# First edge layer of a four-layer graph network: the two column parts of an edge sum resized, and the tail copy placed behind the weighing

## The chip, the cores and the metric

One core of a Trainium2 chip runs the whole program. The metric is the device time of one execution in microseconds. The engines are named as the profile names them: PE is TensorE (PEld its weight loads), DVE is VectorE, ACT is ScalarE, POOL is GpSimd, SP is SyncE.

## The reference

The network has four layers of message passing over 625 nodes and 20000 edges, each followed by a feed-forward or mixture-of-experts part. The change touches the first attention layer of the first of them:

```python
def gatv2(x, src, dst, Ws, bs, Wd, bd, attn):
    H, D = attn.shape                       # 8 heads x 96 here
    fs = (x @ Ws + bs).reshape(-1, H, D)
    fd = (x @ Wd + bd).reshape(-1, H, D)
    e = jax.nn.leaky_relu(fs[src] + fd[dst], 0.2)
    logits = jnp.einsum('ehd,hd->eh', e, attn)
    m = jax.ops.segment_max(logits, dst, num_segments=N)
    ex = jnp.exp(logits - m[dst])
    denom = jax.ops.segment_sum(ex, dst, num_segments=N)
    alpha = ex / denom[dst]
    out = jax.ops.segment_sum(alpha[:, :, None] * fs[src], dst, num_segments=N)
    return jax.nn.elu(out)
```

What concerns us is `logits`: for each edge, the source row and the target row are added (768 columns), passed through a leaky ReLU, multiplied by `attn` and summed in 8 heads of 96 columns.

## The kernel before

The edges are sorted into 181 tiles (`ES`) of up to 128 edges, so that all sources of a tile lie in one block of 125 nodes and all targets in one block. A loop over the 181 tiles computes their logits; it runs twice, once for each of the two attention layers of this part (`first_edges` with g = 0, and `second_edges` with g = 1). Each node row has 776 columns (`GW`): 768 features and 8 columns with a part of the logits that needs no ReLU (the linear 0.2 share, already summed by head). These 8 are called the tail.

One pass of the first loop, for tile i:

- TensorE adds one tally matmul (L826) to a table that counts edges between nodes. Then `node_rows` (L799) picks the source and the target rows with one-hot matrices: four matmuls (two sides, each in a large and a small part) into the PSUM area zA, which holds the last columns with the tail, and four into zB, which holds the first 512 columns. zA shares its PSUM bank with the last part of the tally, so its matmuls always add to what lies there (`first=False`), and it must be cleared before each pass. There is one zA and one zB.
- ScalarE copies the 8 tail columns out of zA (L1272), builds the one-hots of tile i+2 in two steps (`turned_gap`, L1251, the absolute distance of the node number; `turned_onehot`, L1257), and clears zA by copying zeros into it (L1277).
- VectorE weighs the last columns (`weigh_end`, L1725: the larger of 0 and the sum, times the attention vector, into a product buffer), sums the product of the tile before by head (L1735), weighs the first columns from zB (`weigh_start`, L1730), builds a one-hot for every second tile (L1740), and every fourth pass finishes the logits of four tiles (`finish`, L1717).
- GpSimd builds the one-hots of the tally six tiles ahead (L679, L680) and scatters the finished logits to a table in memory (L692). SyncE loads the target numbers of eight tiles at a time, spread over the partitions, into two buffers.

The order is written out by hand for each engine's queue, and semaphores tie the queues: `s_za` counts zA sums, `s_tc` tail copies, `s_wa` weighings of zA, `s_zr` clearings, `s_zp` zB sums, `s_mul` weighings of zB, `s_hd` head sums, `s_tg` gaps and `s_tt` one-hots. The tally matmul of tile i waits for `s_zr` at i; the zB matmuls wait for `s_mul` at i; the tail copy waits for `s_za`; `weigh_end` waits for `s_tc`; the clearing waits for `s_wa`. In the second loop each tile has one of four PSUM areas of two banks, nothing is cleared, and the parts are 384 and 392 columns wide.

Of the kernel before, what the change touches and what calls it, by code (L numbers as in the profile page):

```python
# [14 lines left out]
ALU = mybir.AluOpType  # L15
AX_X = mybir.AxisListType.X

P = 128
# [4 lines left out]
D = 768  # L23
# [7 lines left out]
ES = (E + NQ * (P - 1)) // P  # L31
EW = -(-ES // 4) * 4
HB = D // 2
NB = 16
GW = D + 8
FF = 3072
# [84 lines left out]
def build(nc, ins, out):  # L121
    ctx = ExitStack()
    with ctx:
        def sb(name, shape, dt=F32):
            return ctx.enter_context(nc.sbuf_tensor(name, shape, dt))
# [41 lines left out]
        PB = sb("PB", [P, 3840])  # L167
# [4 lines left out]
        NEG = sb("NEG", [P, T, N])  # L172
# [94 lines left out]
        prod = [WB[:, 2048 + D * b:2048 + D * (b + 1)] for b in range(2)]  # L267
# [35 lines left out]
        PS = ctx.enter_context(nc.psum_tensor("PS", [P, 8, 512], F32))  # L303
        PSz = PS[:, :, :].rearrange("p b n -> p (b n)")
        zw = [PS[:, 2 * b:2 * b + 2, :] for b in range(4)]
        zA = PS[:, 6, P:P + GW - 512]
        zB = PS[:, 7, 0:512]
        tallied = PSz[:, 0:NQ * P]


# [15 lines left out]
        s_za = sem("first_columns_added")  # L326
        s_wa = sem("first_columns_weighed")
        s_tt = sem("turned_onehots_ready")
        s_zp = sem("target_rows_added")
# [24 lines left out]
        s_tc = sem("linear_parts_copied")  # L354
        s_zr = sem("last_columns_cleared")
# [4 lines left out]
        s_mul = sem("edge_products_ready")  # L360
# [401 lines left out]
        def _(pe):  # L762
# [32 lines left out]
            def node_rows(out, i, cd, cs, a, b, first=True):  # L795

                for side, c in ((0, cs), (1, cd)):
                    for part in (large, little):
                        mm = pe.matmul(out, ohT[i % 3][:, (1 - side) * P:(2 - side) * P],  # L799
                                       part[side][:, bass.ds(c, 1), a:b].rearrange("p o n -> p (o n)"),  # L800
                                       start=first, stop=side == 1 and part is little, skip_group_check=True)
                        first = False
                return mm

            def first_edges():

                pe.wait_ge(s_line, 2 * T * 2)
                pe.wait_ge(s_zero, 1)
                for bank in (2, 3, 4, 5, 6, 0, 1):
                    if bank == 0:  # L810
                        pe.wait_ge(s_sorted, 1)
                    if bank == 1:
                        pe.wait_ge(s_idc, 1)
                    pe.matmul(PS[:, bank, :], NEG[:, 0, 0:P], iota[:, 0:512], start=True, stop=False,
                                   skip_group_check=True)
                pe.wait_ge(s_lo, 2 * T)
                now, then = None, blocks_of(0)
                for i in range(ES):
                    if i % 4 == 0:
                        now = then  # L820
                    cs, cd = now[i % 4]
                    wait(pe, s_zr, i)
                    pe.wait_ge(s_oh, i + 1)
                    if i % 2:
                        pe.wait_ge(s_odd, i // 2 + 1)
                    pe.matmul(tallied[:, bass.ds((cd * T + cs) * P, P)], oht[i % 8], ohs[i % 8], start=False,  # L826
                              stop=i == ES - 1, skip_group_check=True).then_inc(s_ohu, 1)
                    pe.wait_ge(s_tt, i + 1)
                    node_rows(zA, i, cd, cs, 512, GW, first=False).then_inc(s_za, 1)
                    if i % 4 == 1 and i // 4 + 1 < EW // 4:  # L830
                        then = blocks_of(i // 4 + 1)
                    wait(pe, s_mul, i)
                    node_rows(zB, i, cd, cs, 0, 512).then_inc(s_zp, 1)
                pe.wait_ge(s_cnt, 1)

            def second_edges():
# [377 lines left out]
        def _(act):  # L1214
# [26 lines left out]
            def edge_parts(g):  # L1241

                chunks = -(-ES // CH)

                def turned_gap(i):
                    q = g * chunks + i // CH
                    if i % CH == 0:
                        act.wait_ge(s_idb[q % 2], 16 * (q // 2 + 1))
                    if i >= 2:
                        act.wait_ge(s_tt, ES * g + i - 1)  # L1250
                    act.activation(tgap[i % 2][0:R], spread_ids[q % 2][0:R, i % CH * 2 * P:(i % CH + 1) * 2 * P],  # L1251
                                   ACT.Abs, bias=node[0:R], scale=-1.0).then_inc(s_tg, 1)

                def turned_onehot(i):
                    act.wait_ge(s_tg, ES * g + i + 1)
                    wait(act, s_zp, ES * g + i - 2)
                    act.activation(ohT[i % 3], tgap[i % 2][0:R], ACT.Relu, bias=ones[0:R, 0:1],  # L1257
                                   scale=-1.0).then_inc(s_tt, 1)

                turned_gap(0)  # L1260
                turned_gap(1)
                turned_onehot(0)
                turned_onehot(1)
                for i in range(ES):
                    if g == 0:
                        act.wait_ge(s_za, i + 1)
                    else:
                        act.wait_ge(s_zp, ES * g + i + 1)
                    if i >= EU:
                        act.wait_ge(s_lg, -(-ES // 4) * g + i // 4 - 2)  # L1270
                    tail = zA[:, D - 512:GW - 512] if g == 0 else zw[i % 4][:, 1, HB:GW - HB]
                    act.copy(tails[:, i % EU, :], tail).then_inc(s_tc, 1)  # L1272
                    if i + 2 < ES:
                        turned_gap(i + 2)
                    if g == 0 and i + 1 < ES:
                        act.wait_ge(s_wa, i + 1)
                        act.copy(zA, NEG[:, 0, 0:GW - 512]).then_inc(s_zr, 1)  # L1277
                    if i + 2 < ES:
                        turned_onehot(i + 2)

            def log_counts(n):
# [219 lines left out]
        def _(dve):  # L1501
# [206 lines left out]
            def finish(g, i):  # L1708

                a, n = i // 4 * 4 % EU, i % 4 + 1  # L1710
                h = HEADS[g]["h"]
                dve.wait_ge(s_hd, ES * g + i + 1)
                for k in range(n):
                    last = i // 4 * 4 + k - EU
                    if last >= 0:
                        dve.wait_ge((s_alt if g else s_sc)[last % SLOTS], 16 * (last // SLOTS + 1))
                dve.scalar_tensor_tensor(out=lgr[:, a:a + n, 0:h], in0=dots[:, a:a + n, 0:h], scalar=-0.8,  # L1717
                                         in1=tails[:, a:a + n, 0:h], op0=ALU.mult, op1=ALU.subtract).then_inc(s_lg, 1)

            def first_edges():  # L1720

                def weigh_end(i):
                    dve.wait_ge(s_tc, i + 1)
                    wait(dve, s_hd, i - 1)
                    dve.scalar_tensor_tensor(out=prod[i % 2][:, 512:D], in0=zA[:, 0:D - 512], scalar=0.0,  # L1725
                                             in1=PB[:, 2 * D + 512:3 * D], op0=ALU.max, op1=ALU.mult).then_inc(s_wa, 1)

                def weigh_start(i):
                    dve.wait_ge(s_zp, i + 1)
                    dve.scalar_tensor_tensor(out=prod[i % 2][:, 0:512], in0=zB, scalar=0.0,  # L1730
                                             in1=PB[:, 2 * D:2 * D + 512], op0=ALU.max, op1=ALU.mult).then_inc(s_mul, 1)

                def head_sums(i):
                    dve.wait_ge(s_mul, i + 1)
                    dve.tensor_reduce(dots[:, i % EU, :], prod[i % 2].rearrange("p (h c) -> p h c", h=8), AX_X, ALU.add)\  # L1735
                       .then_inc(s_hd, 1)

                def odd_targets(i):
                    wait(dve, s_ohu, i - 7)
                    dve.tensor_scalar(oht[i % 8], iota16, idf[:, 1, i:i + 1], None, ALU.is_equal).then_inc(s_odd, 1)  # L1740

                for i in range(1, 6, 2):
                    odd_targets(i)
                for i in range(ES):
                    weigh_end(i)
                    if i:
                        head_sums(i - 1)
                    weigh_start(i)
                    if i % 2 and i + 6 < ES:
                        odd_targets(i + 6)  # L1750
                    if i % 4 == 0 and i:
                        finish(0, i - 1)
                head_sums(ES - 1)
                finish(0, ES - 1)
                counts_out()
                whole_rows(0)
                mask_start()
                mask_end(0)
# [691 lines left out]
```

## Time and profile before

| what | us |
|---|---|
| median of 3 runs | 3249.31 |
| the runs | 3247.78 to 3261.63 |
| span of the profiled execution | 3309.3 |
| mean granted TensorE clock | 0.899 of 2.4 GHz |

The profiled execution is a run of its own, with its own span; all durations of single instructions come from it. In the profile's lists of instructions a line gives engine, source line, operation, the tile written and read, their shapes and the count. A time behind an instruction in square brackets is how long its engine sat idle before it, and what ended that; "issue" means that nothing the profile records explains it. Ends of matmuls are modelled.

### The profile page before, as it was taken

The page shows a single profiled execution, that of the slowest core. Times are in us where ns is not written, and L with a number is a line of the kernel's source. Part 1 is how long each engine was busy: PE and PEld are TensorE (multiplying, and loading weights), DVE is VectorE, ACT ScalarE, POOL GpSimd, SP SyncE. Part 2 cuts the span into 40 slices and gives each one's busy share as a digit, 9 for nine tenths or more (in the row PEclk, how much of TensorE's full clock was granted, in tenths as well). Part 3 has the DMA queues.
Part 4 walks back from the last instruction along what each step waited for, and adds up shares of the span by engine and source line. Part 5 has one row for each costly group of instructions (what it writes and reads, how often), then busy time and mean ns, then how long its engine had stood idle before and what let it go on. Part 6 is the DMA issues. An engine that isn't in the chain of part 4 may idle for free.

```text
span 3309.3 us, 42272 instructions
## 1 busy us (share of the span) xinstructions
PE 2723.5 (82%) x13325; PEld 2178.2 (66%) x13325; DVE 2133.6 (64%) x4348; ACT 1307.6 (40%) x2605; POOL 725.2 (22%) x903
## 2 busy tenths in 40 slices
PE   5879999669888855778998999688857797887998
PEld 3446666555777734678898998547534454766998
DVE  7978888883555546788777777567554235665232
ACT  0036666550555520566555566327110101443110
POOL 4868888300455522000000000200000000000000
PEclk8989999879999975899999999788977798886999
DMA  9601011331211211766656566500000101002120
GB/s 323 197 28 35 28 35 32 97 93 46 46 33 36 34 20 43 257 240 228 207 197 224 172 229 212 204 7 1 15 13 34 44 0 72 15 1 86 58 86 23
DMA packets 72665, 310.35 MB, mean 94 GB/s; under 512 B 22856, under 2 KB 23293, under 8 KB 67258
## 3 DMA queue, kind: packets, MB, share of 16 engines
q1 hardware_dynamic: 51616, 272.78, 25.5%
q0 software_dynamic: 20816, 34.51, 3.3%
q8 instruction: 140, 2.29, 0.3%
q14 instruction: 93, 0.76, 0.1%
HBM read 260.52 MB, written 46.70 MB: 93 GB/s over the span
## 4 chain that ended last, share of the span: by engine, by line
PE 65%; DVE 18%; issue 5%; POOL 5%; ACT 4%; DMA 3%; SPq 0%; another core or an unknown queue 0%; POOLq 0%; DVEq 0%; ACTq 0%
PE PS L799 14%; PE PS L879 10%; PE PS L1126 8%; PE PS L926 7%; PE PS L1023 6%; PE PS L1025 3%; POOL logits L692 2%; PE PS L912 2%; DVE w1s L2076 2%; PE PS L1044 1%; PE PS L1046 1%; PE PS L1045 1%; PE PS L1107 1%; DVE w2s L2081 1%; POOL F L680 1%
## 5 line engine op out<-in xcount | busy, mean ns | idle before, releaser
L799 PE MATMUL PS<-large_rows,turned 125*128 x1448 | 544.6, 379 | 81.2 <-issue 35.2
L799 PE MATMUL PS<-small_rows,turned 125*128 x1448 | 495.8, 346 | 0.0
L692 POOL DMA_INDIRECT logits<-lgr,key x362 | 363.2, 1003 | 338.9 <-DVE lgr L1717 270.9
L1023 PE MATMUL PS<-urowsT,w1s 128*128 128x384 f32 (+2 forms) x1164 | 366.8, 379 | 59.8 <-issue 25.1
L879 PE MATMUL PS<-WB,XT 128*125 128x384 f32 (+1 forms) x1120 | 391.7, 513 | 23.2 <-DMA WB<-in_L_gnn_Wos 12.9
L799 PEld LDWEIGHTS PS<-large_rows,turned 125*128 125x128 f32 x1448 | 274.7, 190 | 169.8 <-issue 155.3
L879 PEld LDWEIGHTS PS<-WB,XT 128*125 128x125 f32 x1120 | 216.1, 194 | 191.9 <-issue 41.9
L926 PE MATMUL PS<-F,PT 125*125 125x96 f32 (+3 forms) x1500 | 298.7, 353 | 18.2 <-ACT PT L1314 8.2
L1025 PE MATMUL PS<-urowsT,w1s 128*128 128x192 f32 (+2 forms) x1164 | 303.3, 261 | 7.1 <-issue 7.1
L1023 PEld LDWEIGHTS PS<-urowsT,w1s 128*128 128x128 f32 x1164 | 229.2, 197 | 92.3 <-issue 58.1
L799 PEld LDWEIGHTS PS<-small_rows,turned 125*128 125x128 f32 x1448 | 274.5, 190 | 8.5
L1768 DVE SCALAR_TENSOR_TENSOR WB<-PS,PB 128x768 f32<-128x768 f32 x181 | 173.4, 958 | 162.4 <-ACT F L1272 145.0
L926 PEld LDWEIGHTS PS<-F,PT 125*125 125x125 f32 x1500 | 236.8, 206 | 60.8 <-issue 18.1
L1126 PE MATMUL PS<-w3s,XT 128*128 128x384 f32 x1440 | 254.9, 339 | 11.1 <-DVE w3s L2169 11.1
L1126 PEld LDWEIGHTS PS<-w3s,XT 128*128 128x128 f32 x1440 | 254.6, 189 | 12.3 <-issue 12.2
L656 POOL TENSOR_TENSOR rstd<-var,mhalf 125x1 f32<-125x1 f32 x50 | 38.2, 764 | 996.9 <-DVE var L1522 996.9
L1025 PEld LDWEIGHTS PS<-urowsT,w1s 128*128 128x128 f32 x1164 | 232.5, 200 | 0.0
L1998 DVE SCALAR_TENSOR_TENSOR X<-PS,comb,X 125x768 f32<-125x768 f32 x70 | 71.2, 1017 | 222.2 <-PE PS L1126 167.2
L2081 DVE TENSOR_TENSOR w2s<-PB,w2s 128x1536 fp32r<-128x1536 f32 x97 | 170.3, 1756 | 40.9 <-ACT w2s L1355 40.9
L912 PE MATMUL PS<-ident,W 125*125 125x125 f32 x650 | 115.2, 317 | 93.1 <-ACT W L1307 92.0
L1251 ACT ACTIVATE O<-WB,node 125x256 f16<-125x256 f16 x362 | 184.7, 511 | 7.0 <-DMA WB<-node_ids 7.0
L1257 ACT ACTIVATE turned<-O,ones 125x256 fp32r<-125x256 f16 x362 | 183.3, 507 | 5.8
(336 smaller groups left out, 4991.4 us busy)
## 6 DMA issues: line engine op xcount, KB each, us to landing
XN<-in_L_ffn_w SPq DMA_DIRECT2D x98, 769.0 KB, 4.3
PB<-in_L_ffn_w SPq DMA_DIRECT2D x97, 768.0 KB, 5.5
WB<-node_ids SPq DMA_DIRECT2D x44, 512.0 KB
logits<-NEG SPq DMA_DIRECT2D x8, 1367.2 KB
WB<-logits SPq DMA_DIRECT2D x5, 2187.5 KB
slot_rows<-NEG POOLq DMA_DIRECT2D x13, 768.0 KB, 55.1
slot_outs<-NEG POOLq DMA_DIRECT2D x12, 768.0 KB, 90.0
C<-in_L_ffn_expert_w SPq DMA_DIRECT2D x8, 1152.0 KB, 5.4
```

What stands on the lines that cost most here:

```text
L692: pool.indirect_dma_start(out=table, out_offset=bass.IndirectOffsetOnAxis(ap=key[:, i:i + 1], axis=0), in_=lgr[:, i % EU, 0:HEADS[g]["h"]] ...
L799: mm = pe.matmul(out, ohT[i % 3][:, (1 - side) * P:(2 - side) * P], part[side][:, bass.ds(c, 1), a:b].rearrange("p o n -> p (o n)"), start ...
L879: mm = pe.matmul(PS[0:R, 4 + g % 4, 0:hw], XT[:, k, t * R:(t + 1) * R], w[:, k, half * hw:(half + 1) * hw], start=(k == 0), stop=(k == kc ...
L912: tr = pe.transpose(PSz[0:R, 1024 * (1 + s % 2) + b * P:1024 * (1 + s % 2) + b * P + R], src[:, b * R:(b + 1) * R], ident[0:R, 0:R])
L926: mm = pe.matmul(PS[0:R, bank, 0:cw], PT[0:R, s % 2, b, :], F[0:R, b, col:col + cw], start=(b == 0), stop=(b == T - 1))
L1023: pe.matmul(both(q % 2, columns), w1s[:, g % 2, 0, w:w + P], urowsT2[:, :, k * TU:k * TU + columns], start=k == 0, stop=False)
L1025: mm = pe.matmul(PS[:, q % 2, 0:columns], w1s[:, g % 2, 1, w:w + P], urowsT2[:, 0, k * TU:k * TU + columns], start=False, stop=k == KD - 1)
L1126: mm = pe.matmul(PS[:, 4 + 2 * ((MB3 + d) % 2) + half, 0:384], XT2[:, a, k, t * R:t * R + P], w3s[:, 2 * u + k // 3, b, col:col + 384], st ...
L1251: act.activation(tgap[i % 2][0:R], spread_ids[q % 2][0:R, i % CH * 2 * P:(i % CH + 1) * 2 * P], ACT.Abs, bias=node[0:R], scale=-1.0).then_ ...
L1257: act.activation(ohT[i % 3], tgap[i % 2][0:R], ACT.Relu, bias=ones[0:R, 0:1], scale=-1.0).then_inc(s_tt, 1)
L1768: dve.scalar_tensor_tensor(out=halves(prod[i % 2]), in0=zw[i % 4][:, :, 0:HB], scalar=0.0, in1=halves(PB[:, 2 * D:3 * D]), op0=ALU.max, op ...
L2081: dve.tensor_tensor(w2s[:, g % 2, 1, :], uw2[g % 2], w2s[:, g % 2, 0, :].bitcast(F32), ALU.subtract).then_inc(s_lo2, 1)
```

## The change

The border between the two parts moves from column 512 to column 392 (`CUT` = 768 + 8 - 384). zA then takes 384 columns (376 features and the tail) where it had 264, and zB 392 where it had 512. In each pass of the first loop, VectorE's `weigh_end` waits for the zA sum itself instead of the tail copy. ScalarE first builds the one-hots of tile i+2, then waits for `weigh_end`, copies the tail, waits for its own copy, and clears zA. `finish` waits for the tail copies as well. The second loop keeps its order on ScalarE.

```diff
+CUT = D + 8 - 384
...
-        zA = PS[:, 6, P:P + GW - 512]
-        zB = PS[:, 7, 0:512]
+        zA = PS[:, 6, P:P + GW - CUT]
+        zB = PS[:, 7, 0:CUT]
...
-                    node_rows(zA, i, cd, cs, 512, GW, first=False).then_inc(s_za, 1)
+                    node_rows(zA, i, cd, cs, CUT, GW, first=False).then_inc(s_za, 1)
...
-                    node_rows(zB, i, cd, cs, 0, 512).then_inc(s_zp, 1)
+                    node_rows(zB, i, cd, cs, 0, CUT).then_inc(s_zp, 1)
...
                 for i in range(ES):
+                    if g == 0 and i + 2 < ES:
+                        turned_gap(i + 2)
+                        turned_onehot(i + 2)
                     if g == 0:
-                        act.wait_ge(s_za, i + 1)
+                        act.wait_ge(s_wa, i + 1)
                     else:
                         act.wait_ge(s_zp, ES * g + i + 1)
...
-                    tail = zA[:, D - 512:GW - 512] if g == 0 else zw[i % 4][:, 1, HB:GW - HB]
+                    tail = zA[:, D - CUT:GW - CUT] if g == 0 else zw[i % 4][:, 1, HB:GW - HB]
                     act.copy(tails[:, i % EU, :], tail).then_inc(s_tc, 1)
-                    if i + 2 < ES:
+                    if g == 0 and i + 1 < ES:
+                        act.wait_ge(s_tc, i + 1)
+                        act.copy(zA, NEG[:, 0, 0:GW - CUT]).then_inc(s_zr, 1)
+                    if g and i + 2 < ES:
                         turned_gap(i + 2)
-                    if g == 0 and i + 1 < ES:
-                        act.wait_ge(s_wa, i + 1)
-                        act.copy(zA, NEG[:, 0, 0:GW - 512]).then_inc(s_zr, 1)
-                    if i + 2 < ES:
                         turned_onehot(i + 2)
...
                 dve.wait_ge(s_hd, ES * g + i + 1)
+                dve.wait_ge(s_tc, ES * g + i + 1)
...
                 def weigh_end(i):
-                    dve.wait_ge(s_tc, i + 1)
+                    dve.wait_ge(s_za, i + 1)
```

The operands of `weigh_end` and `weigh_start` are cut at `CUT` in the same way.

## Rows read from the trace of the kernel before

**Rows 1.** The page's head: span and instructions of the profiled execution.
```profile
span 3309.3 us, 42272 instructions
```

**Rows 2.** Busy time by engine in the first edge loop: PE, PEld, DVE, ACT, POOL; clock; DMA.
```profile
202.90:608.10 405.20, 366.75 (x1621) 246.56 (x1620) 361.36 (x670) 250.80 (x718) 342.32 (x437) 1.00 0.10 30
```

**Rows 3.** Waits in that loop: who waited for whom, total us, times, longest us.
```profile
PEld PS L826 <- issue: 72.9, 180, 0.8
...
DVE WB L1725 <- ACT F L1272: 38.6, 97, 10.2
...
PE PS L826 <- ACT PS L1277: 1.1, 5, 0.4
```

**Rows 4.** Chain of waits through the stretch 200 to 612 us, by line.
```profile
by line: PE PS L799 47.0%; POOL logits L692 16.5%; issue 12.3%; POOL F L680 9.1%; POOL O L679 4.7%; PE PS L826 3.9%; DVE WB L1730 3.3%; DVE WB L1725 1.0%; DMA WB<-node_ids 1.0%; ACT turned L1257 0.7%; DVE dots L1735 0.6%; ACT F L1272 0.3%; 
```

**Rows 5.** Single lines: count, ns (min/median/max), first and last start in us, shapes.
```profile
L1725 DVE SCALAR_TENSOR_TENSOR WB<-PS,PB x181: 424/425/427, 202.9 to 608.1; 128x256 f32<-128x256 f32 x181
...
L1730 DVE SCALAR_TENSOR_TENSOR WB<-PS,PB x181: 679/683/693, 203.7 to 609.3; 128x512 f32<-128x512 f32 x181
...
L1277 ACT COPY PS<-NEG x180: 383/384/385, 203.4 to 606.3; 128x264 f32<-128x264 f32 x180
```

**Rows 6.** Timeline of one pass of the first loop: start us, us, engine, instruction.
```profile
407.54 0.17 ACT L1272 COPY F<-PS 128x8 f32<-128x8 f32 x1 [0.75 <-PE PS L799]
407.61 0.51 ACT L1251 ACTIVATE O<-WB,node 125x256 f16<-125x256 f16 x1
407.74 0.42 DVE L1725 SCALAR_TENSOR_TENSOR WB<-PS,PB 128x256 f32<-128x256 f32 x1 [0.32 <-ACT F L1272]
...
408.20 0.38 ACT L1277 COPY PS<-NEG 128x264 f32<-128x264 f32 x1
...
408.80 0.23 PE L826 MATMUL PS<-F,O 128*128 128x128 bf16 x1
...
408.94 0.68 DVE L1730 SCALAR_TENSOR_TENSOR WB<-PS,PB 128x512 f32<-128x512 f32 x1
408.94 0.39 PE L799 MATMUL PS<-large_rows,turned 125*128 x1
...
409.45 0.29 PE L799 MATMUL PS<-small_rows,turned 125*128 x1
...
409.77 0.49 PE L799 MATMUL PS<-large_rows,turned 125*128 x1
409.77 0.17 ACT L1272 COPY F<-PS 128x8 f32<-128x8 f32 x1 [0.75 <-issue]
...
410.57 0.40 PE L799 MATMUL PS<-small_rows,turned 125*128 x1
```

**Rows 7.** Timeline of the second loop: 384-column matmuls, first and fourth; gap and one-hot.
```profile
1001.61 0.51 ACT L1251 ACTIVATE O<-WB,node 125x256 f16<-125x256 f16 x1
...
1001.81 0.44 PE L799 MATMUL PS<-large_rows,turned 125*128 x1 [0.69 <-ACT turned L1257]
...
1002.15 0.51 ACT L1257 ACTIVATE turned<-O,ones 125x256 fp32r<-125x256 f16 x1
...
1002.44 0.33 PE L799 MATMUL PS<-small_rows,turned 125*128 x1
```

**Rows 8.** Busy time by engine in stretches at either clock level; columns as in group 2.
```profile
837.10:840.20 3.10, 3.10 (x10) 3.10 (x11) 0.00 (x0) 0.11 (x2) 0.00 (x0) 0.50 0.00 0
840.80:843.10 2.30, 2.30 (x14) 2.10 (x12) 1.42 (x4) 1.49 (x4) 0.00 (x0) 1.00 0.00 0
...
2230.00:2233.00 3.00, 1.52 (x7) 0.73 (x5) 0.63 (x1) 1.44 (x3) 0.00 (x0) 1.00 0.00 0
2233.00:2236.00 3.00, 2.81 (x13) 2.81 (x14) 2.90 (x8) 3.00 (x8) 0.00 (x0) 0.56 0.00 0
```

More of the change, by code:

```diff
@@ L1722, in weigh_end @@
                 def weigh_end(i):
-                    dve.wait_ge(s_tc, i + 1)
+                    dve.wait_ge(s_za, i + 1)
                     wait(dve, s_hd, i - 1)
-                    dve.scalar_tensor_tensor(out=prod[i % 2][:, 512:D], in0=zA[:, 0:D - 512], scalar=0.0,
-                                             in1=PB[:, 2 * D + 512:3 * D], op0=ALU.max, op1=ALU.mult).then_inc(s_wa, 1)
+                    dve.scalar_tensor_tensor(out=prod[i % 2][:, CUT:D], in0=zA[:, 0:D - CUT], scalar=0.0,
+                                             in1=PB[:, 2 * D + CUT:3 * D], op0=ALU.max, op1=ALU.mult).then_inc(s_wa, 1)
                 def weigh_start(i):
                     dve.wait_ge(s_zp, i + 1)
-                    dve.scalar_tensor_tensor(out=prod[i % 2][:, 0:512], in0=zB, scalar=0.0,
-                                             in1=PB[:, 2 * D:2 * D + 512], op0=ALU.max, op1=ALU.mult).then_inc(s_mul, 1)
+                    dve.scalar_tensor_tensor(out=prod[i % 2][:, 0:CUT], in0=zB, scalar=0.0,
+                                             in1=PB[:, 2 * D:2 * D + CUT], op0=ALU.max, op1=ALU.mult).then_inc(s_mul, 1)
                 def head_sums(i):
```

## The prediction

> **What bounds the kernel now.** I first located the stage. The change touches only the first edge loop, the 181 passes between VectorE's first and last weighing of the last columns (L1725), which start at 202.9 and at 608.1 us [rows 5]: 405.2 us of a span of 3309.3 us [rows 1], or 405.2 / 180 = 2.251 us from pass to pass. The busy times of just this stretch come next [rows 2]: TensorE 366.75, VectorE 361.36, GpSimd 342.32, ScalarE 250.80 us of 405.20. The reader is to see that three engines are at 84 to 91% and none is full, so a share of busy time doesn't name the limit. The clock granted there is 1.00, the 2.4 GHz level.
>
> The waits of the stretch [rows 3] mislead in two ways. VectorE is seen to wait 38.6 us for ScalarE's tail copy, which looks like a stall that the change removes; 10.2 us of it is one wait, before the first pass. And TensorE seems hardly ever to wait for ScalarE's clearing of zA (L1277): 1.1 us. But the weight load of the tally matmul (L826), the first instruction behind the wait for that clearing, shows 72.9 us of "issue" in 180 passes. The chain of waits [rows 4] puts 47.0% of the stretch on the node-row matmuls, and could be read as a TensorE limit.
>
> What decides is one pass followed in the timeline [rows 6]. Tail copy starts at 407.54; weighing of the last columns 407.74 (+0.20); clearing 408.20 (+0.46); tally matmul 408.80 (+0.60: 0.38 of clearing and 0.22 of hand-over); first zA matmul 408.94 (+0.14); the fourth ends at 409.45 + 0.29 = 409.74 (+0.80); next tail copy 409.77 (+0.03). The sum is 2.23 us, and each step starts 0.02 to 0.22 us behind the end of the one before. This is a **closed ring**: zA has a single buffer, so sum, copy, weigh and clear of one pass come before the sum of the next. 2.23 of the mean 2.251 us is this ring. There is a second ring through zB: weighing of the first columns (408.94, 0.68 long), 0.15 later the zB matmuls (409.77 to 410.57 + 0.40 = 410.97), 0.03, the next weighing: 0.68 + 0.15 + 1.20 + 0.03 = 2.06 us. It is shorter, so it has 0.17 us to spare. VectorE's work alone is 361.36 / 180 = 2.01 us.
>
> **The change part by part.** Columns per pass stay the same (4 x 264 + 4 x 512 before, 4 x 384 + 4 x 392 after); what counts is on which ring they lie.
>
> 1. zA grows from 264 to 384 columns: on the ring. The second edge loop runs the same four operand pairs at 384 columns: the first starts at 1001.81 and the fourth ends at 1002.44 + 0.33 = 1002.77 [rows 7], so 0.96 us against 0.80: **+0.16**.
>
> 2. The weighing of the last columns grows from 256 to 376 columns: on the ring. 256 columns take 425 ns and 512 take 683 [rows 5], 1.008 ns a column: 0.425 + 120 x 0.001008 = 0.546: **+0.12**.
>
> 3. The clearing grows from 264 to 384 columns: on the ring. No row has this shape. Bounds: 0.384 (no growth), and 0.384 x 384 / 264 = 0.559 (all in proportion). Between them lies the slope over ScalarE's two copies, 8 columns in 0.17 [rows 6] and 264 in 0.384 [rows 5]: 0.84 ns a column, so 0.485. I take that one, since part of an instruction is plainly fixed: **+0.10**, bounds 0 to +0.17.
>
> 4. The tail copy is moved from ahead of the weighing to behind it. Before, the ring paid 0.17 + 0.03 from its start to the weighing. After, the weighing waits for the matmuls directly, but the copy now stands between the weighing and the clearing, because ScalarE clears only after its own copy (s_tc), and the copy waits for the weighing (s_wa). The copy is 0.17 again. The wait of ScalarE for its own last instruction is in the trace as gap to one-hot: 1001.61 + 0.51 = 1002.12, then 1002.15 [rows 7], so 0.03. Sum 0.20: **0.00**, bounds -0.03 (no wait) to +0.10 (half of the 0.22 that a hand-over of the clearing to TensorE takes).
>
> 5. The gap and the one-hot of pass i+2 move ahead of the tail copy of pass i. Before, the gap lay under the weighing (407.61 + 0.51 = 408.12, clearing at 408.20): no gain on the ring. After, both follow the clearing: 0.51 + 0.03 + 0.51 = 1.05 us, while ScalarE's next copy is due 0.22 + 0.14 + 0.96 + 0.03 + 0.58 = 1.93 us after the clearing's end. Price nothing; the cover is 0.9 us, and the copy would be late only by what exceeds it. SyncE's loads of spread targets wait for s_tt, which is not reached later within a pass; each holds eight passes, some 20 us. The moved steps issue no DMA themselves. GpSimd's queue (one-hots six passes ahead, scatters) needs 342.32 / 180 = 1.9 us a pass and isn't passed by anything.
>
> 6. VectorE's finish gets a wait for s_tc. The newest tail that it needs was copied one pass earlier, so it ends at once; behind it only the next weighing is queued. In the second layer weighing already waits for the same count: nothing.
>
> 7. zB shrinks from 512 to 392 columns and its weighing with it (0.683 to 0.562): the second ring falls to 0.56 + 0.15 + about 0.96 + 0.03 = 1.70 us. That shortens the ring that did not bind.
>
> New ring: 0.14 + 0.96 + 0.03 + 0.546 + 0.035 (from the weighing to ScalarE, as now) + 0.20 + 0.485 + 0.22 = **2.62 us**. VectorE's work (2.01, unchanged in columns) and the second ring fit inside. TensorE has about 0.6 us idle a pass (zB ends some 0.9 after zA, the tally starts 0.03 + 0.58 + 0.20 + 0.485 + 0.22 = 1.52 after), and this also covers the passes in which reading four block numbers delays zB, which is why I set 2.62 against the mean 2.251 and not against 2.23: 0.369 x 180 = **66 us slower**. Everything behind the loop (counts, the tables of the softmax) waits for its end and just shifts. The span of the profile is 60 us (1.8%) above the median of the runs, 3249.31; a loop shorter by the same share would change the 66 by 1, so I add it to the median: **3315 us**. With the bounds of 3 and 4: 2.49 to 2.79 us, 43 to 97 us, 3292 to 3346.
>
> **The rivals.** *Faster:* VectorE sets the pace, and its wait for the tail copy goes. For: 38.6 us of that wait, 28.4 without the first [rows 3]. It gives 3249 - 28 = 3221. It decides only if zA of the next pass is summed before VectorE is free, that is if the ring falls below VectorE's 2.01 us; against it, the copy stays in the ring and the ring is 2.62.
>
> *No change:* TensorE is the limit, as the chain's 47.0% suggests [rows 4]; its columns are the same, so 3249. Against: its matmuls of a pass take 0.14 + 0.80 + 1.20 = 2.14 at most, and the tally begins 0.22 after the clearing, not at the end of zB. The change could also miss the point in this way if clearing were not waited for; the code waits (s_zr).
>
> *Much slower:* the clock falls, since TensorE now idles 0.6 us in every pass. The 1.2 GHz level is seen behind a long idle: 3 us with TensorE busy for only 1.52 of them at clock 1.00 are followed by 3 us at 0.56 [rows 8]. Matmuls of 384 columns then take 3.10 / 10 = 0.31 against 2.30 / 14 = 0.16 us [rows 8], so a zA four costs 0.6 us more; were half of the passes at this level, 90 x 0.6 = 54, 3369 us. Against: that drop followed some 1.5 us without work, over twice as long. The Trainium skill bears on this one, in TensorE: Matmul & The Clock Gate, "A second HAM failure mode: psum-queue depth-cycling": there TensorE's short idles between groups of matmuls made the clock swing between its levels. By that the time would be this rival's, not the forecast's; the trace of this loop so far shows no such swing at 1.00 throughout [rows 2].
>
> **How the numbers follow.** Forecast 0.80, faster 0.06, no change 0.06, clock 0.08. The forecast is the likeliest, 3315, and its own bounds, 3292 to 3346, hold the 0.80 that the range wants. About 0.5% (16 us) is what a measurement of this kernel can tell from no change; all of the forecast and the clock rival lie above that: slower 0.88, same 0.06, faster 0.06.
>
> **What would show it.** In the profile after: L1725 from first to last start over some 471 us; its mean 546 ns, the clearing's 485; tail copy right behind the weighing and clearing 0.20 behind that; VectorE idle about 0.6 us a pass, now waiting for TensorE; zB's weighing never waiting; clock 1.00. It is wrong if the loop's length stays (then the ring was not the limit), if passes last 2.62 but the end doesn't move, or if the clock of the loop falls.

## The result and the profile after

| | before | after |
|---|---|---|
| median of 4 runs each, us | 3254.86 | 3320.68 |
| the runs, us | 3247.78 to 3261.63 | 3313.5 to 3332.42 |
| ratio, 95% interval | 1 | 1.0205 (1.0171 to 1.0239) |
| span of the profiled execution, us | 3309.3 | 3330.6 |

The change makes the kernel 2.05% slower: 65.8 us between the medians, where 66 us were predicted. (The predicted 3315 us counted them from 3249.31, the median of the three runs known then; a fourth run of the kernel before raises it to 3254.86.)

It lies in the first edge loop. Its instructions as single lines (count, ns as minimum/median/maximum, first and last start in us, shapes), after the change, and the busy time of the stretch (PE, PEld, DVE, ACT, POOL, then clock and DMA):

```profile
L1729 DVE SCALAR_TENSOR_TENSOR WB<-PS,PB x181: 548/549/552, 201.8 to 676.2; 128x376 f32<-128x376 f32 x181
...
L1734 DVE SCALAR_TENSOR_TENSOR WB<-PS,PB x181: 553/555/566, 202.6 to 677.5; 128x392 f32<-128x392 f32 x181
...
L1279 ACT COPY PS<-NEG x180: 482/483/485, 202.6 to 674.4; 128x384 f32<-128x384 f32 x180
```
```profile
201.80:676.20 474.40, 341.38 (x1622) 258.92 (x1621) 381.04 (x670) 285.75 (x717) 342.73 (x437) 1.00 0.08 25
```

The loop takes 676.2 - 201.8 = 474.4 us, 2.636 us a pass, where [rows 5] gave 405.2 and 2.251: 69.2 us more. TensorE, at 366.75 of 405.20 us before [rows 2], is now busy for 341.38 of 474.40: it has become idler, not busier, with the clock still at 1.00. One pass of the new loop in the timeline answers to [rows 6]:

```profile
407.35 0.55 DVE L1729 SCALAR_TENSOR_TENSOR WB<-PS,PB 128x376 f32<-128x376 f32 x1
...
407.93 0.17 ACT L1276 COPY F<-PS 128x8 f32<-128x8 f32 x1 [0.96 <-DVE WB L1729]
408.13 0.48 ACT L1279 COPY PS<-NEG 128x384 f32<-128x384 f32 x1
408.55 0.50 ACT L1252 ACTIVATE O<-WB,node 125x256 f16<-125x256 f16 x1
...
408.83 0.23 PE L827 MATMUL PS<-F,O 128*128 128x128 bf16 x1 [0.81 <-ACT PS L1279]
...
408.97 0.44 PE L800 MATMUL PS<-large_rows,turned 125*128 x1
409.08 0.51 ACT L1258 ACTIVATE turned<-O,ones 125x256 fp32r<-125x256 f16 x1
...
409.60 0.34 PE L800 MATMUL PS<-small_rows,turned 125*128 x1
...
409.98 0.55 DVE L1729 SCALAR_TENSOR_TENSOR WB<-PS,PB 128x376 f32<-128x376 f32 x1 [0.74 <-PE PS L800]
```

The ring can be read off again: weighing to tail copy 0.58, copy to clearing 0.20, clearing to tally 0.70 (0.48 and a hand-over of 0.22), tally to the first zA matmul 0.14, to the end of the fourth 409.94 - 408.97 = 0.97, to the next weighing 0.04: 2.63 us. The gap and the one-hot (408.55 and 409.08) lie behind the clearing and end at 409.59, long before the next copy. The waits of this stretch (who for whom, total us, times, longest) now say plainly what [rows 3] hid:

```profile
PE PS L827 <- ACT PS L1279: 121.9, 180, 0.8
...
DVE WB L1729 <- PE PS L800: 98.9, 145, 9.9
...
DVE WB L1734 <- PE PS L800: 0.2, 1, 0.2
```

TensorE waits for the clearing in each of 180 passes. Before, only 1.1 us of that wait was shown, because TensorE was still at zB's matmuls when the clearing ended. Measured from row to row, the tally follows the clearing's end by 0.22 us in all 180 passes after the change. Before, it did so in 135; in the other 45, the passes in which TensorE also reads four block numbers and starts zB late, it came 0.32 to 0.50 us behind. So the ring was closed before the change in three passes of four.

The spans differ by 21.3 us only, not by 69. Most of the rest is the second edge loop, whose code is the same: in the trace of before it took 334 us, in that of after 292 us. The first experiment asks which of them is the rule.

### The profile page after: what moved, and what is told of

Its sections match the earlier page's. It is cut to its first block, busy times and chain, and to the rows that moved or that the text cites. A ratio compares the mean times of both kernels' runs of the same rounds, so it can differ in the third digit from the quotient of the medians.

```text
span 3330.6 us, 42362 instructions
## 1 busy us (share of the span) xinstructions
PE 2688.3 (81%) x13325; PEld 2185.6 (66%) x13325; DVE 2153.0 (65%) x4348; ACT 1346.1 (40%) x2605; POOL 723.0 (22%) x903
## 4 chain that ended last, share of the span: by engine, by line
PE 53%; DVE 19%; POOL 9%; issue 9%; ACT 5%; DMA 5%; SPq 0%; POOLq 0%; DVEq 0%; ACTq 0%
PE PS L880 9%; PE PS L1127 8%; POOL logits L693 6%; PE PS L927 6%; PE PS L1024 6%; PE PS L800 4%; PE PS L1026 3%; DVE WB L1729 2%; PE PS L913 2%; ACT PS L1279 2%; DVE w1s L2080 2%; DMA logits<-lgr,key 2%; PE PS L1045 1%; PE PS L1047 1%; PE PS L1046 1%
## 5 line engine op out<-in xcount | busy, mean ns | idle before, releaser
L800 PE MATMUL PS<-large_rows,turned 125*128 x1448 | 529.8, 366 | 29.1 <-issue 21.1
L1127 PEld LDWEIGHTS PS<-w3s,XT 128*128 128x128 f32 x1440 | 254.4, 189 | 12.3 <-issue 12.2
```

The costliest lines, as they stand in the source:

```text
L1127: mm = pe.matmul(PS[:, 4 + 2 * ((MB3 + d) % 2) + half, 0:384], XT2[:, a, k, t * R:t * R + P], w3s[:, 2 * u + k // 3, b, col:col + 384], st ...
```

## The experiments

**The kernel before, once more.** No edit.

> The kernel before once more, for its stages: in the recorded traces the first edge loop took 405 us before and 474 after (+69), but the spans differ by 21 only, because the second edge loop, whose code is the same, took 334 us in the trace of before and 292 in that of after. Theory: the second loop's length varies from execution to execution, and its 42 us are no work of the change; then this run may show about 292 us there and a span near 3265, with a first loop of 405. Rival: the change shortened the second loop; then it is 334 again and the span is near 3309.

The span was 3258.7 us. The second loop by its first and last weighing, in the first trace of before, in this one and in that of after (columns as above, one row from each trace):

```profile
840.30:1174.50 334.20, 290.79 (x1440) 249.70 (x1438) 175.95 (x404) 190.29 (x538) 169.09 (x176) 0.98 0.18 34
```
```profile
838.70:1130.30 291.60, 281.27 (x1440) 245.00 (x1438) 177.31 (x404) 193.98 (x538) 168.59 (x176) 1.00 0.25 39
```
```profile
907.00:1198.80 291.80, 281.40 (x1440) 244.81 (x1438) 177.34 (x404) 194.02 (x538) 168.58 (x176) 1.00 0.23 39
```

The same instructions take 334.2 us in one execution of the kernel before and 291.6 in another. VectorE's, ScalarE's and GpSimd's busy times agree within 2%; TensorE's is 290.79 against 281.27, at a clock of 0.98 against 1.00. In the traces of all later runs below the loop takes 290.5 to 292.2 us. So the second loop's 42 us are no work of the change, and most of the 60 us by which the first trace stood above the median lie there. The first loop took 405.2 us in both traces. Why the second loop ran slowly in that one execution is open.

**The cut alone.** The new cut, everything else as before:

```diff
+CUT = D + 8 - 384
-        zA = PS[:, 6, P:P + GW - 512]
-        zB = PS[:, 7, 0:512]
+        zA = PS[:, 6, P:P + GW - CUT]
+        zB = PS[:, 7, 0:CUT]
...
                     act.copy(tails[:, i % EU, :], tail).then_inc(s_tc, 1)
                     if i + 2 < ES:
                         turned_gap(i + 2)
                     if g == 0 and i + 1 < ES:
                         act.wait_ge(s_wa, i + 1)
```

> Only the new cut (384 and 392 columns), the tail copy still ahead of the weighing and the gap between copy and clearing, as in the kernel before. Theory (the ring through zA sets the pass, and the place of the copy in it is worth nothing): 0.03 + 0.20 + 0.58 + 0.48 + 0.22 + 0.14 + 0.97 = 2.62 us a pass, loop 472 us, some 66 us slower than before. Rival (the copy's new place behind the weighing is what costs): a pass of 2.25, no change.

```profile
L1726 DVE SCALAR_TENSOR_TENSOR WB<-PS,PB x181: 548/549/551, 202.1 to 676.4; 128x376 f32<-128x376 f32 x181
```

The loop took 474.3 us, the whole change 474.4. The ratio to the kernel before is 1.0178 (1.0133 to 1.0223), 3319.88 us. The cut brings the entire loss; at this cut the order is worth nothing.

**The order alone.** The changed kernel with the old border:

```diff
-CUT = D + 8 - 384
+CUT = 512
```

> Only the new order (weighing on the sum, then tail copy, then clearing; one-hots ahead of both), with the old cut of 512 and 264 columns. Theory: 0.04 + 0.425 + 0.035 + 0.20 + 0.38 + 0.22 + 0.14 + 0.80 = 2.24 us a pass, loop 403 us, no change within 0.5%. Rival (the order costs): up to 2.62 and 66 us slower. Second rival (the tail wait was a real stall on VectorE): 2.03 a pass, 38 us faster.

```profile
L1729 DVE SCALAR_TENSOR_TENSOR WB<-PS,PB x181: 408/424/426, 201.8 to 619.3; 128x256 f32<-128x256 f32 x181
...
L1744 DVE TENSOR_SCALAR O<-XT,idf x90: 242/659/757, 191.3 to 605.5; 128x128 bf16<-128x128 f16 x90
```

None of the three: the loop took 417.5 us, 12.3 more than before; the ratio is 1.0037 (1.0011 to 1.0063). So at the old cut the new order is not free. The second of these rows shows a suspect. VectorE's one-hot of odd tiles, which stands right ahead of the weighing of zA, takes 659 ns in the median where it took 246 in the kernel before. In the timeline of the order alone, and then of the kernel before:

```profile
302.89 1.04 POOL L693 DMA_INDIRECT logits<-lgr,key  x1 [0.17 <-issue]
...
303.27 0.66 DVE L1744 TENSOR_SCALAR O<-XT,idf 128x128 bf16<-128x128 f16 x1
```
```profile
301.38 1.05 POOL L692 DMA_INDIRECT logits<-lgr,key  x1 [0.17 <-issue]
301.57 0.25 DVE L1740 TENSOR_SCALAR O<-XT,idf 128x128 bf16<-128x128 f16 x1
```

Begun 0.38 us into GpSimd's scatter, the one-hot ends with it, at 303.93; begun 0.19 into it, it takes its 0.25. Two later runs take this up.

**No clearing.** The changed kernel with zA's matmuls overwriting; the zeros copy and with it the counts of the last block pair are left out:

```diff
-                    wait(pe, s_zr, i)
+                    wait(pe, s_tc, i)
...
-                    node_rows(zA, i, cd, cs, CUT, GW, first=False).then_inc(s_za, 1)
+                    node_rows(zA, i, cd, cs, CUT, GW).then_inc(s_za, 1)
...
-                    if g == 0 and i + 1 < ES:
-                        act.wait_ge(s_tc, i + 1)
-                        act.copy(zA, NEG[:, 0, 0:GW - CUT]).then_inc(s_zr, 1)
```

> The changed kernel without the clearing of zA: its matmuls overwrite, TensorE waits for the tail copy instead; the zeros copy is left out, so the counts of the last block pair are not kept. Theory: the ring loses 0.48 and a hand-over: 2.63 - 0.48 - 0.03 = 2.12 us a pass, loop 381 us, about 92 us less than the changed kernel. Rival (TensorE or VectorE set the pass and the clearing lies beside it, as the waits of before would have it): 2.6 a pass, no change against the changed kernel.

```profile
L1726 DVE SCALAR_TENSOR_TENSOR WB<-PS,PB x181: 548/550/552, 202.0 to 592.3; 128x376 f32<-128x376 f32 x181
```

The loop took 390.3 us, 84.1 less than with the clearing (92 were expected; 2.17 us a pass instead of 2.12), and the kernel 3244.51. TensorE and VectorE still run the same 1621 and 670 instructions in it, so neither had set the pass: the clearing had, as a link of the ring. Passes of 2.12 us, as expected, and of 2.22 us take turns; what holds up the longer ones is taken up under *The tail copy off the ring*.

**A cut half way.** The changed kernel with zA at 324 columns:

```diff
-CUT = D + 8 - 384
+CUT = D + 8 - 324
```

> The changed kernel with zA at 324 columns, half way between 264 and 384 (zB 452). Theory (each column of zA costs on the ring): zA 0.88, weighing of 316 columns 0.49, clearing 0.43: a pass of 2.43 us, loop 438 us, about 36 us less than the changed kernel. Rival (a threshold, or zB's ring taking over): 474 or 417 again.

```profile
L1729 DVE SCALAR_TENSOR_TENSOR WB<-PS,PB x181: 473/487/490, 201.4 to 637.1; 128x316 f32<-128x316 f32 x181
...
L1279 ACT COPY PS<-NEG x180: 432/433/435, 202.2 to 635.4; 128x324 f32<-128x324 f32 x180
```

435.7 us, against 438 expected, and 38.7 less than at 384 columns. The clearing took 384, 433 and 483 ns at 264, 324 and 384 columns: 0.82 ns a column, close to the 0.84 that step 3 chose between its bounds. No threshold shows between these cuts.

**The tail copy off the ring.** The kernel before with the copy reading a tile of zeros, so that the weighing needn't wait for it; the tails are left out of the first layer's logits:

```diff
-                    tail = zA[:, D - 512:GW - 512] if g == 0 else zw[i % 4][:, 1, HB:GW - HB]
+                    tail = NEG[:, 0, 0:8] if g == 0 else zw[i % 4][:, 1, HB:GW - HB]
...
 def weigh_end(i):
-    dve.wait_ge(s_tc, i + 1)
+    dve.wait_ge(s_za, i + 1)
```

> The kernel before with the tail copy taken from a tile of zeros, so that it no longer reads zA and VectorE weighs on the sum itself; the tails are left out of the first layer's logits. Theory: the ring of 2.23 loses the copy's 0.20 and becomes 2.03, so zB's ring (2.06) and VectorE's work (2.01) set the pass: loop about 375 us, 30 us less than before. Rival (the copy's place in the ring is worth nothing since other limits lie just beneath): 395 to 405.

```profile
L1726 DVE SCALAR_TENSOR_TENSOR WB<-PS,PB x181: 409/424/427, 201.4 to 591.9; 128x256 f32<-128x256 f32 x181
```

390.5 us: 14.7 less than before, half of the 30 expected. The copy was a link of the ring, but a next limit lies at about 2.17 us a pass, above the 2.06 of zB's ring and the 2.01 of VectorE's work that I had put there. The run without clearing stopped at the same 2.17. The traces show the same engine behind both, GpSimd. Its waits in the kernel before, in the run without clearing and in this one:

```profile
POOL logits L692 <- DVE lgr L1717: 36.5, 43, 15.8
POOL logits L692 <- issue: 23.2, 133, 0.3
```
```profile
POOL logits L693 <- issue: 30.2, 174, 0.2
POOL logits L693 <- DVE lgr L1718: 15.1, 1, 15.1
```
```profile
POOL logits L692 <- issue: 29.6, 171, 0.2
POOL logits L692 <- DVE lgr L1718: 15.5, 1, 15.5
```

Before, GpSimd waited 43 times for VectorE's finished logits. In the two faster loops it waits for them once, at the start, and then never rests longer than the 0.17 us or so that lie ahead of each scatter. Two passes of its work, from the timeline of the run without clearing:

```profile
399.83 1.03 POOL L693 DMA_INDIRECT logits<-lgr,key  x1 [0.18 <-issue]
...
404.17 1.04 POOL L693 DMA_INDIRECT logits<-lgr,key  x1 [0.17 <-issue]
```

That is 4.34 us for two passes, 2.17 for one. Each tally waits for GpSimd's one-hot of its tile: without the clearing that one-hot ends 0.33 us ahead of the tally in every second pass, where in the kernel before it was ready at least 0.97 us ahead. In the run with the copy off the ring the passes in which TensorE reads four block numbers start zB 0.4 us late and take 2.39 us, but the others make up for it at 2.04 to 2.13. No run made GpSimd's part shorter with the copy or the clearing gone, so this limit is read from the traces and not tried.

**The order alone, odd one-hot moved.** The new order with the old cut, and VectorE's one-hot behind the weighing of zA instead of ahead of the next one:

```diff
                     weigh_end(i)
+                    if i % 2 and i + 6 < ES:
+                        odd_targets(i + 6)
                     if i:
                         head_sums(i - 1)
                     weigh_start(i)
-                    if i % 2 and i + 6 < ES:
-                        odd_targets(i + 6)
```

> The new order with the old cut, and VectorE's one-hot of odd tiles moved from behind the weighing of zB to behind the weighing of zA. In the run of the order alone its rows took 637 ns instead of 249, each ending with GpSimd's scatter instruction, and the loop took 417 us instead of the 403 of the ring. Theory (VectorE is held up by GpSimd there): with rows back near 250 ns the loop falls to 403 to 406; if they are still long, the loop stays long. Rival (the order itself costs 12 us): rows of 250 ns and a loop of 417.

```profile
L1729 DVE SCALAR_TENSOR_TENSOR WB<-PS,PB x181: 423/425/427, 201.8 to 607.0; 128x256 f32<-128x256 f32 x181
...
L1744 DVE TENSOR_SCALAR O<-XT,idf x90: 243/549/756, 191.5 to 591.5; 128x128 bf16<-128x128 f16 x90
```

The loop is back at 405.2 us, the length of the kernel before (ratio 1.0012, 0.9994 to 1.0030), though the one-hot is still slow (549 ns). Both halves of what I had expected fall short: the duration doesn't decide alone. What decides is whether the one-hot stands between VectorE's last work and the weighing that the ring waits for.

**The order alone, no scatter.** The same order and cut, GpSimd's scatters of the first loop left out, so that the first layer's logits are not stored:

```diff
+                if g == 0:
+                    pool.nop().then_inc(done, 16)
+                    return
                 pool.indirect_dma_start(
```

> The order alone (old cut) once more, with GpSimd's scatters of the first loop left out, so the first layer's logits are not stored. It tells apart why the order alone took 417 us and not 403. Theory: VectorE's one-hot of odd tiles was held up by the scatter (637 ns against 249); without scatters its rows are 249 ns and the loop takes 403 to 406. Rival: the tail copy used to run while VectorE was still late with that one-hot and now stands behind the weighing, whatever GpSimd does; then the rows are 249 ns and the loop still takes 411 to 417.

```profile
L1732 DVE SCALAR_TENSOR_TENSOR WB<-PS,PB x181: 408/424/427, 202.0 to 613.0; 128x256 f32<-128x256 f32 x181
...
L1747 DVE TENSOR_SCALAR O<-XT,idf x90: 239/246/453, 191.5 to 599.4; 128x128 bf16<-128x128 f16 x90
```

The one-hot is at 246 ns again, and the loop takes 411.0 us: between the two theories. Of the 12.3 us that the order costs at the old cut, 6.5 go with the scatter, and 5.8 stay without it. Both parts lie in one pass of four, the one in which TensorE reads four block numbers, zB starts late and VectorE is late with it: 2.26 us in the kernel before, 2.55 with the order alone, 2.40 without the scatter, while the other three take 2.23 to 2.25 in all three traces. The second part is the rival's, as far as the runs show: before, the tail copy ran while VectorE was still finishing its one-hot, so in such passes the copy's 0.20 us cost nothing; behind the weighing it comes on top.

**The tail in zB.** The kernel before with zA holding the first 300 columns, zB the other 476 with the tail, the copy taken from zB while VectorE sums by head:

```diff
+CUT = 300
-        zA = PS[:, 6, P:P + GW - 512]
-        zB = PS[:, 7, 0:512]
+        zA = PS[:, 6, P:P + CUT]
+        zB = PS[:, 7, 0:GW - CUT]
...
+                    if g == 0 and i + 1 < ES:
+                        act.wait_ge(s_wa, i + 1)
+                        act.copy(zA, NEG[:, 0, 0:CUT]).then_inc(s_zr, 1)
+                    act.wait_ge(s_zp, ES * g + i + 1)
...
+                    tail = zB[:, D - CUT:GW - CUT] if g == 0 else zw[i % 4][:, 1, HB:GW - HB]
...
 def weigh_start(i):
-    dve.wait_ge(s_zp, i + 1)
+    dve.wait_ge(s_tc, i + 1)
```

> A version that takes the tail out of zA's ring: zA holds the first 300 columns, zB the other 476 with the tail; ScalarE copies the tail from zB while VectorE is still at the head sums, and VectorE weighs zB after that. Theory: zA's ring 0.04 + 0.47 + 0.035 + 0.42 + 0.22 + 0.14 + 0.85 = 2.17 us, zB's ring 0.64 + 0.15 + 1.13 + 0.03 + 0.20 = 2.15 us: loop about 391 us, 14 us less than before, 0.4% faster. Rival (VectorE's order, with the one-hot of odd tiles held up by GpSimd's scatter, sets the pass): 405 to 417, no change or slower.

```profile
L1722 DVE SCALAR_TENSOR_TENSOR WB<-PS,PB x181: 456/470/473, 202.0 to 600.9; 128x300 f32<-128x300 f32 x181
```

398.9 us, 6.3 less than before, where 14 were expected; the ratio is 0.9981 (0.9966 to 0.9995), 3245.87 against 3249.23 us. It is the fastest of the versions that compute everything, by 0.1% between these medians and 0.2% by the ratio over the runs. Three passes of four take 2.13 to 2.18 us, about the 2.17 expected; those in which TensorE reads four block numbers take 2.42.

**The tail in zB, two more moves.** TensorE reads the block numbers ahead of its wait for the clearing, and the odd one-hot stands behind the weighing of zA:

```diff
+                    if i % 4 == 1 and i // 4 + 1 < EW // 4:
+                        then = blocks_of(i // 4 + 1)
                     wait(pe, s_zr, i)
...
                     weigh_end(i)
+                    if i % 2 and i + 6 < ES:
+                        odd_targets(i + 6)
...
-                    if i % 2 and i + 6 < ES:
-                        odd_targets(i + 6)
```

> The version with the tail in zB (399 us in the first loop), with two more moves: TensorE reads the four block numbers ahead of its wait for the clearing, so that every fourth zB no longer starts 0.36 us late, and VectorE's one-hot of odd tiles stands behind the weighing of zA. Theory: all passes become like its shorter ones, 2.13 to 2.17 us: loop 384 to 391 us, 14 to 21 us less than before, 0.4 to 0.6% faster. Rival (VectorE's own work is the floor that it met): loop of 399 as without the moves.

```profile
L1722 DVE SCALAR_TENSOR_TENSOR WB<-PS,PB x181: 449/470/472, 202.1 to 607.9; 128x300 f32<-128x300 f32 x181
```

A miss: 405.8 us, longer than without the two moves, and 0.9986 (0.9968 to 1.0003) for the kernel. The timeline shows one reason, in a pass with the reading (clearing, then tally):

```profile
401.08 0.41 ACT L1268 COPY PS<-NEG 128x300 f32<-128x300 f32 x1 [0.20 <-DVE WB L1722]
...
402.19 0.23 PE L829 MATMUL PS<-F,O 128*128 128x128 bf16 x1 [0.25 <-issue]
```

The clearing ends at 401.49 and the tally starts 0.70 later, where 0.22 is the rule: the reading was taken off zB's ring and put on zA's. One pass of four now takes 2.54 us where it took 2.42, and the other three are as they were, at 2.15 to 2.17. The other move did no good either: behind the weighing of zA the one-hot falls into the scatter. Its rows without the two moves, and then with them:

```profile
L1737 DVE TENSOR_SCALAR O<-XT,idf x90: 243/246/766, 191.6 to 587.8; 128x128 bf16<-128x128 f16 x90
```
```profile
L1737 DVE TENSOR_SCALAR O<-XT,idf x90: 240/671/744, 191.5 to 593.0; 128x128 bf16<-128x128 f16 x90
```

No run has one move without the other, so their shares are not shown. The lower end of the 384 to 391 us expected was out of reach anyway if GpSimd needs 2.17 us a pass, 391 us in 180 passes.

## Why the prediction was right, step by step

- **What bounds the kernel**: right. Taking one link out of the ring shortens the loop (no clearing: 84 us; the copy off the ring: 15 us), and lengthening its links lengthens it by their sum, while TensorE's columns stay the same. "TensorE is the limit" and "VectorE waits for the copy" were both readings of true rows [rows 3, 4] that name no limit. Two things were simpler in the working than in the trace. The ring of 2.23 us closes 135 of the 180 passes before the change; in the other 45 TensorE comes late from zB. And not every step of the ring starts behind the end of the one before: zA's first matmul starts 0.14 us after the start of the tally, which takes 0.23. The sum uses the 0.14, so it stands.
- **Step 1, zA's matmuls**: +0.16 forecast, 0.97 - 0.80 = 0.17 measured. **Step 2, weighing**: 0.546 forecast, 0.549 measured. **Step 3, clearing**: 0.485 forecast between bounds of 0.384 and 0.559, 0.483 measured.
- **Step 4, the moved copy**: 0.00 forecast. At the new cut that holds (cut alone 474.3, whole change 474.4 us), and 0.20 us between copy and clearing is what the trace shows. It isn't a general price: at the old cut the order costs 12.3 us in the loop. The step named the ring alone. It left out that VectorE, ahead of the weighing, was at times later than the sum, and that the copy had been hidden there. With 384 columns VectorE has time to spare, so nothing of this shows.
- **Step 5, gap and one-hot**: right; both end 0.97 us before the copy (409.59 and 410.56 in the timeline of after). The 1.9 us a pass that the step gives GpSimd is its busy time alone; with the pauses ahead of its scatters it needs 2.17, as the two faster loops show. At 2.62 us a pass that changes nothing.
- **Steps 6 and 7**: right; the weighing of zB waited 0.2 us in all.
- **The sum**: 2.62 us a pass forecast; the timeline's pass is 2.63, the mean 2.636. The loop is 69.2 us longer, 66 were forecast; the medians differ by 65.8. That the medians meet the forecast to 0.2 us is luck: the interval of the ratio reaches from 56 to 78 us.
- **The span against the median**: this step failed in its reason. I spread the 60 us between span and median over the whole kernel; 42.6 of them (334.2 - 291.6) sat in the second edge loop of that one execution. The first loop had its usual 405.2, so the sum was not touched, but the spans alone would have shown a loss of 21 us.
- **The rivals**: *faster* needed a ring below VectorE's pace; even with the copy off the ring at the old cut the gain was 14.7 us, not 28; by the traces the floor there is GpSimd's 2.17 us a pass and not VectorE's 2.01, which the rival took for it. *No change* fell with the ring. *The clock* stayed at 1.00 through the loop, with TensorE idle for 474.40 - 341.38 = 133 us of it in pieces of under 1 us.

## What to carry to other kernels

Where a buffer is single, follow one pass from its filling to its release and add the links: a stall that the waits list as large may be a link that merely moves, and the wait that matters may hide under "issue" or under work still queued ahead of it. Columns are worth different amounts by the ring on which they lie: the same 776 columns cost 69 us more a loop when 120 of them moved from a ring with time to spare to the one that closes. The next limit can be an engine that looks less busy: count the pauses that it always makes along with its work, as with GpSimd's 0.17 us ahead of each scatter. Compare stages, not spans, between two traces, and run the old kernel again before its stages are used as a yardstick.

## What the runs showed of the hardware

A small VectorE instruction, a 128x128 comparison from 16-bit to 16-bit in SBUF, takes 246 ns by itself and up to 770 beside GpSimd's scatter of 1.04 us. With the scatters left out the median is 246 again. Over all the traces with scatters, none of the 295 begun in the first 0.26 us of a scatter was held, the one shown at 0.19 among them; of the 351 begun between 0.27 and 0.76 us into it, 349 ended with it, like the one at 0.38, and two were held for part of it. The Trainium skill has a rule on this in SBUF — State Buffer, "Who interferes with whom": VectorE and GpSimd share a pair of ports under an exclusive lock, and whoever issues first has it for the whole instruction. The rows agree that VectorE is held up to the end of GpSimd's instruction. They differ on the start: the scatter was always there first, yet it did not keep out a comparison begun in its first 0.26 us. That it is these ports which hold VectorE up is the Trainium skill's account; no run here tells it from another. What such a hold-up costs depended on its place: 6.5 us a loop right ahead of the weighing, nothing that shows behind it.

The second edge loop, unchanged, took 334.2 us in one execution and 290.5 to 292.2 in the eleven others that were traced. The cause is open.
